# Layer 1's edge stage: float32 one-hots for the expansion of the destinations' scores, and constant products on TensorE

## The chip, the cores and the metric

One core of one Trainium2 chip runs the whole kernel. The metric is the device time of one execution in microseconds; the time of before is the median of three executions. A measurement of this kernel tells a difference from none at about 0.2%.

## What is computed

The kernel is two layers of a graph network over 6250 nodes and 106250 edges, each layer with experts behind it. The change lies in the graph attention of the second layer (layer 1, eight heads, 32 channels each):

```python
alpha = a_src[src] + a_dst[dst] + a_edge
alpha = leaky_relu(alpha, 0.2)
m = segment_max(alpha, dst)
ea = exp(alpha - m[dst])
den = segment_sum(ea, dst)
msg = xp[src] * (ea / den[dst])
out = segment_sum(msg, dst)
```

The edges are sorted by destination. `a_dst[dst]` is what the change computes in another way.

## The kernel before

The stages of the kernel run one after the other. `stage_l1_edges` (line 2312) takes the edges in 58 rounds of 16 steps (`R`) of 128 edges. Every engine runs its own program over the rounds, in the order in which it is written out by hand, and they meet only at semaphores.

- **GpSimd (POOL)**, line 2471: one indirect DMA per step gathers the rows of the 128 sources (256 values with a one for each head, 264 in all, and 8 scores) into `got`, a ring of three rounds. Before each fourth gather it waits until the sums of the same steps three rounds earlier are done (`summed`), which frees their part of the ring.
- **ScalarE (ACT)** makes one-hot matrices: `hot_t` (lines 2495 and 2499, four pieces of 128x512 a round, bfloat16) has the destination node on the partitions, `hot` (lines 2487 and 2482, float32) the edge.
- **TensorE (PE)** does four kinds of products. `expand` (line 2710) gives every edge its destination's score: `hot_t` times `parts`, 16 a round, in four pieces. `parts` are the scores `to_dst` split into three bfloat16 numbers (`split_in_three`, once at the start), so each product has 24 columns. `sums` (line 2721) adds the weighted rows by destination, 16 a round in four pieces, float32, 264 columns. `hop` 0 to 3 (lines 2729, 2732, 2735, 2740 and 2742) are the small products and transposes on the path of the segment maximum.
- **VectorE (DVE)**: `score` (lines 2576 to 2585) adds the three scores of a round: `base`, the sum over the three parts (`from_dst`, line 2579), the addition (line 2582), the leaky ReLU (line 2585, `one`). `spans`, `chains` and `differences` compute the maxima; `weigh` (line 2628) multiplies the gathered rows of four steps by their weights; `add` (line 2636) takes the sums from PSUM.

The rounds are interleaved on TensorE: in its round p stand the hops of round p, the sums of round p-1 and the expansion for round p+1:

```python
hop_of(0)
sums_of(0)
expand_of(0)
hop_of(1)
sums_of(1)
expand_of(1)
hop_of(2)
sums_of(2)
expand_of(2)
expand_of(3)
sums_of(3)
hop_of(3)
```

Hop 0 waits for `one`, hop 1 for `ends` (the end of `spans`), hop 2 for `c_top` (in `chains`), hop 3 for VectorE and for the exponentials of ScalarE; it gives the weights for which the next round's first `weigh` waits. `sums_of(b)` waits for `weigh(b)`. Layer 0 has an edge stage of the same build (`stage_l0_edges`, line 1188; gathers in line 1372) with the same 928 gathers; the change leaves it alone.

Of the kernel before, what the change touches and what calls it, by code (L numbers as in the profile page):

```python
# [19 lines left out]
BF16 = mybir.dt.bfloat16  # L20
I32 = mybir.dt.int32
ALU = mybir.AluOpType
# [1891 lines left out]
def split_in_three(dve, link, whole, parts):  # L1914

    for k in range(2):
        link.done(dve.tensor_copy(parts[k], whole))
        link.done(dve.tensor_tensor(whole, whole, parts[k], ALU.subtract))
    return dve.tensor_copy(parts[2], whole)
# [392 lines left out]
def stage_l1_edges(nc, T, K, acc):  # L2312
# [10 lines left out]
    with ExitStack() as ctx:  # L2323
# [9 lines left out]
        parts = s.sb("parts", [P, NT, 3, H], BF16)  # L2333
        apart = s.sb("apart", [P, 3, R, P], BF16)
        hot = s.sb("hot", [P, 3, U, P])
        hot_t = s.sb("hot_t", [P, B4, U * P], BF16)
# [12 lines left out]
        from_dst = s.sb("from_dst", [P, R, H])  # L2349
# [21 lines left out]
        pa = s.ps("pa", [P, SUMS, 512])  # L2371
        p_one, p_chain, p_tops = px[:, 0:P], px[0:H, P:P + 2 * R], px[:, 2 * P:2 * P + 2 * R]
# [4 lines left out]
        parts_ready = s.sem("parts_ready")  # L2377
# [172 lines left out]
        def _(dve):  # L2550
            link = Tally(dve, s.sem("dve"))
            link.done(dve.memset(links[:, :, :], -BIG))
# [6 lines left out]
            link.done(split_in_three(dve, link, to_dst[:, :, :], [parts[:, :, k, :] for k in range(3)]))  # L2559
            dve.sem_inc(parts_ready, 1)  # L2560
# [10 lines left out]
            def score(p, k, turn, pair):  # L2571
                dve.wait_ge(got_in[k], 16 * R * (turn + 1))
                if isinstance(p, int) and p == 0:
                    dve.wait_ge(edge_in, 16)
                for n in range(RS):
                    ins = dve.tensor_tensor(base[:, 2 * n:2 * n + 2, :], got[:, k, 2 * n:2 * n + 2, WV:ROW],
                                            edge[:, bass.ds(pair[n] * 2, 2), :], ALU.add)
                dve.wait_ge(expanded, B4 * (p + 1))
                dve.tensor_reduce(from_dst[:, :, :], pd[:, 0:R * 3 * H].rearrange("p (r k h) -> p r h k", k=3, h=H), AX, ALU.add
                                  ).then_inc(dst_taken, 1)  # L2580
                dve.wait_ge(dst_taken, p + 1)
                dve.tensor_tensor(base[:, :, :], base[:, :, :], from_dst[:, :, :], ALU.add).then_inc(based, 1)
                dve.wait_ge(based, p + 1)
                flat = base[:, :, :].rearrange("p r h -> p (r h)")
                dve.scalar_tensor_tensor(one[:, :], flat, 0.2, flat, ALU.mult, ALU.max).then_inc(one_ready, 1)
# [115 lines left out]
        def _(pe):  # L2701
            pe.wait_ge(parts_ready, 1)

            def expand(p, b, tile):
                pe.wait_ge(hot_t_ready, p * B4 + b + 1)
                if b == 0 and not (isinstance(p, int) and p == 0):
                    pe.wait_ge(dst_taken, p)
                for u in range(U):
                    r = b * U + u
                    mm = pe.matmul(pd[:, r * 3 * H:(r + 1) * 3 * H], hot_t[:, b, u * P:(u + 1) * P],  # L2710
                                   parts[:, bass.ds(tile[r // 2], 1), :, :].rearrange("p a k h -> p (a k h)"), start=True, stop=True)
                mm.then_inc(expanded, 1)
# [31 lines left out]
            def round_(p, k, ahead, now_, behind):  # L2744
# [14 lines left out]

                hop_of(0)  # L2760
                sums_of(0)
                expand_of(0)
                hop_of(1)
                sums_of(1)
                expand_of(1)
                hop_of(2)
                sums_of(2)
                expand_of(2)
                expand_of(3)
                sums_of(3)  # L2770
                hop_of(3)
# [1110 lines left out]
```

## Time and profile before

| | |
|---|---|
| median of three executions | 7020.55 us (7016.5 to 7024.07) |
| the profiled execution: its time, its span | 7091.8 us, 7089.9 us |
| TensorE clock granted, mean over the span | 0.798 |
| first and last gather of layer 1's edge stage | 4483.7 us, 5879.6 us |
| first and last leaky ReLU of its rounds (L2585) | 4522.8 us, 5892.9 us |
| last sum taken from PSUM (L2636) | 5918.1 us |

The profiled execution is 71 us (1.0%) above the median of the executions that were only timed. Times in rows are microseconds from the start of the span unless marked ns. A row of a timeline begins with start and duration; at its end stands in brackets how long the engine sat idle before it and what released it. A product of float32 operands leaves two records on PE and two weight loads on PEld, one of bfloat16 leaves one of each. The granted clock is 1.0 at 2.4 GHz and 0.5 at 1.2 GHz.

### The profile page before, as it was taken

Reading aid. Unit: us, or ns where it says so; the run is one execution under the profiler, and the core shown is the slowest. Engines: PE = TensorE matmul, PEld = TensorE weight load, DVE = VectorE, ACT = ScalarE, POOL = GpSimd, SP = SyncE. Lnnn points to the kernel's source line nnn. Section 1 sums busy time; section 2 is a strip of 40 time slices with the busy share of each in tenths; the row PEclk is TensorE's granted clock in tenths of the full one; section 3 lists DMA queues with packets and bytes.
Section 4 is the critical chain, followed back from the end, with each engine's and each line's share of the span. In section 5 each row is a group of like instructions: output and inputs, shape, how many; then the busy total and the mean of one; then the engine's idle time right before and its main releaser. Section 6 shows DMA issues by size and latency. Waiting matters only on the chain. (4 is left out here: it accounts for less than half of the span.)

```text
span 7089.9 us, 85593 instructions
## 1 busy us (share of the span) xinstructions
PE 4861.7 (69%) x21453; PEld 3465.5 (49%) x21454; DVE 3989.0 (56%) x9527; ACT 2604.5 (37%) x4956; POOL 3069.3 (43%) x3260
## 2 busy tenths in 40 slices
PE   4368375777777787477778734355555556999999
PEld 3246134555565577345555523244444434666565
DVE  4248136999999975411221297466666666445443
ACT  0134003555555532033333331355555552222222
POOL 2641605666666567366666400466666661000000
PEclk6568697999989955588898856677777777999999
DMA  1001147888888776322222215444444442000000
GB/s 50 1 0 30 48 161 232 251 248 246 250 247 251 237 188 148 96 62 62 59 54 64 59 58 181 139 125 126 126 126 126 123 126 79 11 10 10 10 10 11
DMA packets 587384, 787.20 MB, mean 111 GB/s; under 512 B 207700, under 2 KB 427323, under 8 KB 586749
## 3 DMA queue, kind: packets, MB, share of 16 engines
q0 software_dynamic: 159136, 383.90, 20.3%
q1 hardware_dynamic: 290173, 351.82, 15.6%
q10 hardware_dynamic: 137972, 50.36, 3.1%
q8 instruction: 34, 0.56, 0.0%
q14 instruction: 69, 0.57, 0.0%
HBM read 634.22 MB, written 158.32 MB: 112 GB/s over the span
## 5 line engine op out<-in xcount | busy, mean ns | idle before, releaser
L1372 POOL DMA_INDIRECT b_got<-tmp_l_table,b_src x928 | 877.5, 946 | 537.7 <-issue 251.8
L2471 POOL DMA_INDIRECT w_got<-tmp_l_table,w_src x928 | 879.4, 948 | 519.6 <-issue 261.1
L3203 POOL DMA_INDIRECT t_got<-tmp_f_table,t_src x672 | 634.2, 944 | 409.8 <-DVE t_sums L3281 204.8
L2721 PE MATMUL w_pa<-w_got,w_hot 128*128 128x264 f32 x1856 | 654.3, 512 | 206.1 <-DVE w_got L2628 111.0
L1616 PE MATMUL b_pk<-b_keys,b_hot_t 128*128 x1856 | 553.0, 450 | 284.9 <-issue 194.8
L2721 PEld LDWEIGHTS w_pa<-w_got,w_hot 128*128 128x128 f32 x1856 | 444.2, 252 | 325.4 <-issue 228.7
L1616 PEld LDWEIGHTS b_pk<-b_keys,b_hot_t 128*128 128x128 f32 x1856 | 388.4, 220 | 379.7 <-issue 320.1
L3654 DVE SCALAR_TENSOR_TENSOR l_accs<-l_po,l_prob,l_accs 128x256 f32 (+1 forms) x392 | 173.5, 480 | 564.1 <-PE l_po L3763 564.1
L3706 ACT ACTIVATE l_h<-l_ph,l_bn 128x896 f32<-128x896 f32 x224 | 245.0, 1096 | 652.9 <-PE l_ph L3753 652.9
L3325 PE MATMUL t_po<-t_w,t_hid 128*128 128x256 f32 x1568 | 411.2, 412 | 107.0 <-issue 76.4
L1631 PE MATMUL b_pa<-b_got,b_hot 128*128 128x260 f32 x1856 | 476.8, 402 | 7.8 <-DVE b_acc L1543 4.9
L3317 PE MATMUL t_ph<-t_xt,t_w 128*128 128x448 f32 x896 | 395.4, 585 | 72.7 <-issue 60.1
L1631 PEld LDWEIGHTS b_pa<-b_got,b_hot 128*128 128x128 f32 x1856 | 376.5, 205 | 87.4 <-issue 20.0
L3325 PEld LDWEIGHTS t_po<-t_w,t_hid 128*128 128x128 f32 x1568 | 315.4, 206 | 171.9 <-issue 113.8
L3753 PE MATMUL l_ph<-l_xt,l_wm 128*128 128x448 f32 x896 | 360.5, 558 | 29.6 <-ACT l_h L3706 29.2
L3753 PE MATMUL l_ph<-l_h,l_wm 128*128 128x448 f32 x896 | 356.6, 552 | 2.3 <-DVE l_logit L3622 2.3
L3763 PE MATMUL l_po<-l_wm,l_h 128*128 128x256 f32 x1568 | 348.1, 379 | 8.8 <-ACT l_h L3706 8.8
L1385 ACT ACTIVATE b_hot_t<-b_spread,const_minus_col 128x512 f32<-128x512 bf16 x232 | 166.1, 716 | 508.2 <-remote 351.1
L3763 PEld LDWEIGHTS l_po<-l_wm,l_h 128*128 128x128 f32 x1568 | 296.9, 190 | 67.1 <-issue 27.6
L2628 DVE TENSOR_TENSOR w_got<-w_got,w_pwf 128x1056 f32<-128x1056 f32 x232 | 289.8, 1249 | 56.6 <-remote 47.5
L3243 ACT ACTIVATE t_hid<-t_ph,t_b 128x896 f32<-128x896 f32 x112 | 112.1, 1005 | 534.6 <-remote 307.2
L1475 DVE TENSOR_TENSOR b_got<-b_pk,b_got 128x1024 f32<-128x1024 f32 x232 | 282.6, 1218 | 44.2 <-remote 33.1
(577 smaller groups left out, 9915.5 us busy)
## 6 DMA issues: line engine op xcount, KB each, us to landing
tmp_g_acc<-b_acc SPq DMA_DIRECT2D x232, 260.0 KB
b_spread<-tmp_g_rel_rows SPq DMA_DIRECT2D x116, 256.0 KB
w_spread<-tmp_g_rel_rows SPq DMA_DIRECT2D x116, 256.0 KB
e_attr<-in_edge_attr ACTq DMA_DIRECT2D x103, 256.0 KB
tmp_f_experts<-t_y SPq DMA_DIRECT2D x28, 896.0 KB
t_spread<-tmp_f_rel_rows SPq DMA_DIRECT2D x174, 128.0 KB
yl_y<-tmp_f_experts SPq DMA_DIRECT2D x20, 896.0 KB, 11.1
b_got<-tmp_l_table,b_src POOLq DMA_INDIRECT x928
```

The lines of the kernel that those rows point to most:

```text
L1372: pool.indirect_dma_start(out=got[:, m % NB, u, :], out_offset=None, in_=T["l0_table"], in_offset=bass.IndirectOffsetOnAxis(ap=src[:, m * ...
L1475: dve.tensor_tensor(q, pk[:, b % 2, :].rearrange("p (u d) -> p u d", u=U), q, ALU.mult).then_inc(multiplied, 1)
L1616: mm = pe.matmul(pk[:, b % 2, u * D:(u + 1) * D], hot_t[:, (at * B4 + b) % HB, u * P:(u + 1) * P], keys[:, bass.ds(tile[u // 2], 1), :], s ...
L1631: mm = pe.matmul(pa[:, n % 2, 0:WV], hot[:, b, v, :], got[:, k, v, D:ROW], start=(u == 0), stop=(u == 1))
L2471: pool.indirect_dma_start(out=got[:, p % 3, u, :], out_offset=None, in_=T["l1_table"], in_offset=bass.IndirectOffsetOnAxis(ap=src[:, p * R ...
L2628: dve.tensor_tensor(rows, rows, w.unsqueeze(3).broadcast_to((P, U, H, V)), ALU.mult).then_inc(rhs_ready, 1)
L2721: mm = pe.matmul(pa[:, (k * RS + n) % SUMS, 0:WV], hot[:, (k * B4 + b) % 3, u - b * U, :], got[:, k, u, 0:WV], start=(u == 2 * n), stop=(u ...
L3203: pool.indirect_dma_start(out=got[:, g % RING, u, :], out_offset=None, in_=T["f_table"], in_offset=bass.IndirectOffsetOnAxis(ap=src[:, g * ...
L3317: mm = pe.matmul(ph[:, f % 2, half, 0:HALF], w1[:, e, a, f * P:(f + 1) * P], xt[:, a, half * HALF:(half + 1) * HALF], start=(a == 0), stop ...
L3325: mm = pe.matmul(po[:, f % 2, t % 2, :], hid[:, e % 2, a, t * P:(t + 1) * P], w2[:, e, a, :], start=(a == 0), stop=(a == FC - 1))
L3753: mm = pe.matmul(ph[:, f, h, 0:HALF], wm[which][:, e, a, f * P:(f + 1) * P], of[:, a, h * HALF:(h + 1) * HALF], start=(a == 0), stop=(a == 1))
L3763: mm = pe.matmul(slot(t), h2[:, e % 2, f, t * P:(t + 1) * P], wm[2][:, e, f, :], start=(f == 0), stop=(f == 1))
```

## The change

It has two parts.

The expansion works on float32 throughout: `hot_t` is a float32 tile, the products take `to_dst` itself as the moving operand (8 columns instead of 24), and `parts`, its splitting at the start and `from_dst` go. VectorE adds the result from PSUM to `base` in one operation where it had a reduction and an addition; the semaphore `based` is signalled after the first additions instead.

And TensorE gets products of a constant bfloat16 tile of ones (`idle`, 128x128 against 128x512) into a PSUM bank of their own, `p_idle`, which nobody reads. `fill(n)` issues n of them; they wait for nothing and signal nothing. By the calls in `round_` there are 13 of them in a round (2, 2, 1, 2, 1, 2, 2 and 1), in each of TensorE's 60 rounds.

```diff
-        parts = s.sb("parts", [P, NT, 3, H], BF16)
-        hot_t = s.sb("hot_t", [P, B4, U * P], BF16)
+        hot_t = s.sb("hot_t", [P, B4, U * P])
-        from_dst = s.sb("from_dst", [P, R, H])
+        p_idle = s.ps("p_idle", [P, 512])
+        idle = s.sb("idle", [P, 512], BF16)
...
+            dve.memset(idle[:, :], 1.0).then_inc(idle_ready, 1)
-            link.done(split_in_three(dve, link, to_dst[:, :, :], [parts[:, :, k, :] for k in range(3)]))
-            dve.sem_inc(parts_ready, 1)
...
+                ins.then_inc(based, 1)
                 dve.wait_ge(expanded, B4 * (p + 1))
-                dve.tensor_reduce(from_dst[:, :, :], pd[:, 0:R * 3 * H].rearrange("p (r k h) -> p r h k", k=3, h=H), AX, ALU.add
+                dve.wait_ge(based, p + 1)
+                dve.tensor_tensor(base[:, :, :], base[:, :, :], pd[:, 0:R * H].rearrange("p (r h) -> p r h", h=H), ALU.add
                                   ).then_inc(dst_taken, 1)
                 dve.wait_ge(dst_taken, p + 1)
-                dve.tensor_tensor(base[:, :, :], base[:, :, :], from_dst[:, :, :], ALU.add).then_inc(based, 1)
-                dve.wait_ge(based, p + 1)
...
-            pe.wait_ge(parts_ready, 1)
+            pe.wait_ge(idle_ready, 1)
+            pe.wait_ge(loaded, 8 * 16)
+            def fill(n):
+                for _ in range(n):
+                    pe.matmul(p_idle[:, :], idle[:, 0:P], idle[:, :], start=True, stop=True)
...
-                    mm = pe.matmul(pd[:, r * 3 * H:(r + 1) * 3 * H], hot_t[:, b, u * P:(u + 1) * P],
-                                   parts[:, bass.ds(tile[r // 2], 1), :, :].rearrange("p a k h -> p (a k h)"), start=True, stop=True)
+                    mm = pe.matmul(pd[:, r * H:(r + 1) * H], hot_t[:, b, u * P:(u + 1) * P],
+                                   to_dst[:, bass.ds(tile[r // 2], 1), :].rearrange("p a h -> p (a h)"), start=True, stop=True)
...
+                fill(2)
                 hop_of(0)
+                fill(2)
                 sums_of(0)
                 expand_of(0)
+                fill(1)
                 hop_of(1)
+                fill(2)
                 sums_of(1)
                 expand_of(1)
+                fill(1)
                 hop_of(2)
+                fill(2)
                 sums_of(2)
                 expand_of(2)
                 expand_of(3)
+                fill(2)
                 sums_of(3)
+                fill(1)
                 hop_of(3)
```

On TensorE, from the start of round 1 to hop 1, before the change (a row is a line of the kernel, the operation, its tiles and its shape; x4 is four in a row; a product is one row whatever records it leaves; in the compiled order `w_` marks tiles of this stage, and the `ISA` row sets an address):

```order
L2415 TENSOR_LOAD w_i_row
L2729 MATMUL w_px<-const_ident,w_one 128x128
L2721 MATMUL w_pa<-w_got,w_hot 128x264 x4
L2710 ISA
L2710 MATMUL w_pd<-w_parts,w_hot_t 128x24 x2
L2710 ISA
L2710 MATMUL w_pd<-w_parts,w_hot_t 128x24 x2
L2732 MATMUL w_px<-w_ends,w_of_head 8x32
```

And after it:

```order
L2415 TENSOR_LOAD w_i_row
L2707 MATMUL w_p_idle<-w_idle 128x512 x2
L2734 MATMUL w_px<-const_ident,w_one 128x128
L2707 MATMUL w_p_idle<-w_idle 128x512 x2
L2726 MATMUL w_pa<-w_got,w_hot 128x264 x4
L2715 ISA
L2715 MATMUL w_pd<-w_to_dst,w_hot_t 128x8 x2
L2715 ISA
L2715 MATMUL w_pd<-w_to_dst,w_hot_t 128x8 x2
L2707 MATMUL w_p_idle<-w_idle 128x512
L2737 MATMUL w_px<-w_ends,w_of_head 8x32
```

Five products of `w_idle` stand on the way from the load of the tiles' numbers to hop 1, and the four products of the expansion have 8 columns instead of 24.

On TensorE, at the end of the same round, from the last pair of expansion products to hop 3, before:

```order
L2710 ISA
L2710 MATMUL w_pd<-w_parts,w_hot_t 128x24 x2
L2721 MATMUL w_pa<-w_got,w_hot 128x264 x4
L2740 MATMUL w_pwf<-w_fade_mat,w_first_hot 128x8
L2742 MATMUL w_pwf<-const_ident,w_exps 128x128
```

And after it:

```order
L2715 ISA
L2715 MATMUL w_pd<-w_to_dst,w_hot_t 128x8 x2
L2707 MATMUL w_p_idle<-w_idle 128x512 x2
L2726 MATMUL w_pa<-w_got,w_hot 128x264 x4
L2707 MATMUL w_p_idle<-w_idle 128x512
L2745 MATMUL w_pwf<-w_fade_mat,w_first_hot 128x8
L2747 MATMUL w_pwf<-const_ident,w_exps 128x128
```

Between `sums_of(2)` and `hop_of(3)` stand three constant products more, and ahead of them eight expansion products in the new form, of which the last two are shown.

On VectorE, in `score`, from the last addition of `base` to the leaky ReLU and the first `weigh`, before:

```order
L2576 ISA
L2576 TENSOR_TENSOR w_base<-w_got,w_edge 128x16
L2579 TENSOR_REDUCE w_from_dst<-w_pd 128x128
L2582 TENSOR_TENSOR w_base<-w_base,w_from_dst 128x128
L2585 SCALAR_TENSOR_TENSOR w_one<-w_base 128x128
L2628 TENSOR_TENSOR w_got<-w_got,w_pwf 128x4x264
```

And after it:

```order
L2575 ISA
L2575 TENSOR_TENSOR w_base<-w_got,w_edge 128x16
L2580 TENSOR_TENSOR w_base<-w_base,w_pd 128x128
L2584 SCALAR_TENSOR_TENSOR w_one<-w_base 128x128
L2627 TENSOR_TENSOR w_got<-w_got,w_pwf 128x4x264
```

The reduction from PSUM is gone, and the addition that is left reads PSUM itself.

## Rows read from the trace of the kernel before

**Rows 1.** The page: span, busy time by engine, one of its costliest groups.

```profile
span 7089.9 us, 85593 instructions
...
PE 4861.7 (69%) x21453; PEld 3465.5 (49%) x21454; DVE 3989.0 (56%) x9527; ACT 2604.5 (37%) x4956; POOL 3069.3 (43%) x3260
...
L1385 ACT ACTIVATE b_hot_t<-b_spread,const_minus_col 128x512 f32<-128x512 bf16 x232 | 166.1, 716 | 508.2 <-remote 351.1
```

**Rows 2.** Windows in three stages (layer 0 edges, layer 1 edges, last experts).

```profile
core 0: us, PE busy (x) PEld busy (x) DVE busy (x) ACT busy (x) POOL busy (x), PEclk, DMA share, GB/s
1400.00:1600.00 200.00, 150.66 (x602) 115.06 (x600) 183.87 (x334) 109.66 (x250) 125.72 (x133) 0.93 0.82 247
5200.00:5400.00 200.00, 109.61 (x474) 80.23 (x474) 122.56 (x366) 109.58 (x250) 125.44 (x133) 0.74 0.46 126
6000.00:6200.00 200.00, 193.47 (x655) 122.36 (x654) 99.32 (x248) 52.84 (x55) 0.00 (x0) 0.97 0.03 10
```

**Rows 3.** Groups of layer 1's edge stage: busy us, mean ns, idle before.

```profile
L2471 POOL DMA_INDIRECT w_got<-tmp_l_table,w_src x915 | 867.2, 948 | 513.7 <-issue 257.5 <-PE w_pa L2721 129.4 <-remote 126.8
...
L2721 PEld LDWEIGHTS w_pa<-w_got,w_hot 128*128 128x128 f32 x1856 | 444.2, 252 | 325.4 <-issue 228.7 <-DVE w_got L2628 8.6
...
L2499 ACT ACTIVATE w_hot_t<-w_spread,const_ones 128x512 bf16<-128x512 bf16 x232 | 167.4, 722 | 38.2 <-DMA e_attr<-in_edge_attr 8.9 <-issue 8.8 <-ACT w_spread L2495 1.5
...
L2710 PEld LDWEIGHTS w_pd<-w_parts,w_hot_t 128*128 128x128 bf16 x928 | 57.6, 108 | 84.3 <-issue 61.9
...
L2579 DVE TENSOR_REDUCE w_from_dst<-w_pd 128x128 f32<-128x384 f32 x58 | 32.3, 557 | 30.4 <-DMA e_attr<-in_edge_attr 29.4 <-issue 0.9
...
L2740 PE MATMUL w_pwf<-w_fade_mat,w_first_hot 8*128 8x8 f32 x116 | 23.2, 270 | 0.0
...
L2582 DVE TENSOR_TENSOR w_base<-w_base,w_from_dst 128x128 f32<-128x128 f32 x58 | 17.0, 293 | 2.0
...
L2590 DVE TENSOR_TENSOR w_now<-w_px,w_early 128x128 f32<-128x128 f32 x58 | 16.3, 281 | 14.6 <-issue 14.5
...
L1917 DVE CAST w_parts<-w_to_dst 128x392 bf16<-128x392 f32 x2 | 1.1, 560 | 0.2
```

**Rows 4.** Gathers of layer 0: line 1372, and the first after its ring had filled.

```profile
L1372 POOL DMA_INDIRECT b_got<-tmp_l_table,b_src x928: 940/946/1112, 1057.8 to 2469.8; - x186
...
1153.00 0.94 POOL L1372 DMA_INDIRECT b_got<-tmp_l_table,b_src  x1 [35.41 <-PE b_pa L1631]
```

**Rows 5.** Gathers of layer 1: line 2471 as a whole.

```profile
L2471 POOL DMA_INDIRECT w_got<-tmp_l_table,w_src x928: 940/946/1129, 4483.7 to 5879.6; - x186
```

**Rows 6.** GpSimd's timeline in layer 1's stage: each gather after a wait, one without.

```profile
4561.88 0.94 POOL L2471 DMA_INDIRECT w_got<-tmp_l_table,w_src  x1 [18.29 <-PE w_pa L2721]
...
5304.49 0.95 POOL L2471 DMA_INDIRECT w_got<-tmp_l_table,w_src  x1 [2.19 <-PE w_pa L2721]
5305.74 0.94 POOL L2471 DMA_INDIRECT w_got<-tmp_l_table,w_src  x1 [0.30 <-issue]
...
5316.38 0.94 POOL L2471 DMA_INDIRECT w_got<-tmp_l_table,w_src  x1 [2.21 <-remote]
...
5328.24 0.94 POOL L2471 DMA_INDIRECT w_got<-tmp_l_table,w_src  x1 [2.07 <-PE w_pa L2721]
```

**Rows 7.** Timeline of TensorE and VectorE at the end of one round.

```profile
5309.78 0.35 PE L2710 MATMUL w_pd<-w_parts,w_hot_t 128*128 x8
...
5309.99 2.03 PE L2721 MATMUL w_pa<-w_got,w_hot 128*128 128x264 f32 x8
...
5311.86 0.43 DVE L2636 TENSOR_TENSOR l_sums<-l_sums,w_pa 128x264 f32 x1 [0.46 <-PE w_pa L2721]
...
5311.95 0.38 PE L2740 MATMUL w_pwf<-w_fade_mat,w_first_hot 8*128 8x8 f32 x2
...
5316.34 0.43 DVE L2636 TENSOR_TENSOR l_sums<-l_sums,w_pa 128x264 f32 x1 [4.06 <-remote]
```

**Rows 8.** Timeline pieces: hop 3, `weigh`, a piece of `sums` at either clock, hop 2.

```profile
5197.43 0.38 PE L2740 MATMUL w_pwf<-w_fade_mat,w_first_hot 8*128 8x8 f32 x2
...
5197.74 0.33 PE L2742 MATMUL w_pwf<-const_ident,w_exps 128*128 128x128 f32 x1
...
5198.81 1.25 DVE L2628 TENSOR_TENSOR w_got<-w_got,w_pwf 128x1056 f32<-128x1056 f32 x1
...
5200.19 2.04 PE L2721 MATMUL w_pa<-w_got,w_hot 128*128 128x264 f32 x8 [0.92 <-issue]
...
5225.58 3.88 PE L2721 MATMUL w_pa<-w_got,w_hot 128*128 128x264 f32 x8 [0.77 <-issue]
...
5237.00 0.63 PE L2735 MATMUL w_px<-w_c_top,w_to_head 8*128 8x32 f32 x2 [4.87 <-DVE w_c_top L2603]
```

**Rows 9.** Two 512-column bfloat16 products of the sort stage: timeline, then the line.

```profile
227.55 0.60 PE L637 MATMUL s_pq<-s_not_below,s_ident 128*128 128x512 bf16 x2
...
L637 PE MATMUL s_pq<-s_not_below,s_ident x128: 379/390/634, 126.0 to 665.5; 128*128 128x512 bf16 x128
```

More of the change, by code:

```diff
@@ L2371, in stage_l1_edges @@
         pa = s.ps("pa", [P, SUMS, 512])
+        p_idle = s.ps("p_idle", [P, 512])
+        idle = s.sb("idle", [P, 512], BF16)
+        idle_ready = s.sem("idle_ready")
         p_one, p_chain, p_tops = px[:, 0:P], px[0:H, P:P + 2 * R], px[:, 2 * P:2 * P + 2 * R]
@@ L2376, in stage_l1_edges @@
         set_up = s.sem("set_up")
-        parts_ready = s.sem("parts_ready")
         spread_in = [s.sem(f"spread_in{h}") for h in range(2)]
```

## The prediction

> **What bounds the kernel now.** I read the views from the whole to the place. The page has no engine at its limit: TensorE is busy for 69% of the span, VectorE for 56%, GpSimd for 43% [rows 1], so the limit has to be read stage by stage. The windows of three stages show that [rows 2]. In the last experts' stage TensorE is busy for 193.47 of 200 us; the change does not touch it. In the edge stage of layer 1 nobody is near his limit: TensorE 109.61, VectorE 122.56, ScalarE 109.58, GpSimd 125.44 us of 200, at a granted clock of 0.74, so TensorE moves between its two levels.
>
> The reader should then compare the first two windows. In layer 0's edge stage VectorE is busy for 183.87 us and TensorE's clock is at 0.93; in layer 1's they are 122.56 and 0.74. Both have 133 gathers on GpSimd in 200 us. The exact pace says the same. A ring holds 48 gathers, and the first gather that had to wait for it starts at 1153.00 in layer 0 and at 4561.88 in layer 1; the last of the 928 start at 2469.8 and 5879.6 [rows 4, 5, 6]. That is (2469.8 - 1153.00) / 879 = 1.498 us a gather in the one stage and (5879.6 - 4561.88) / 879 = 1.499 us in the other, or 24.0 us a round, although the work behind the gathers differs. Without a wait gathers start 1.25 us apart [rows 6], which would be 20.0 us a round; the rest is waiting for TensorE's sums, (129.4 + 126.8) / 58 = 4.4 us a round [rows 3].
>
> The timelines show what kind of wait this is. GpSimd stops after eight gathers for some 2.1 us and the pieces are 11.89 and 11.86 us long, 1.48 us a gather [rows 6]. At the end of one of them TensorE's last piece of sums ends at 5312.02, the second take of VectorE begins only at 5316.34, after 4.06 us of idling, and GpSimd's gather at 5316.38 [rows 7]. Products that the trace has as finished are thus seen by VectorE and by GpSimd 4.3 us later, both at once, when GpSimd has been standing still. I can't say from the rows what holds the signals back. But it goes on while gathers are being issued, and then neither a faster TensorE nor a faster VectorE shortens it.
>
> **The change part by part.** Durations are from the profiled execution (7091.8 us, 1.0% above the median of 7020.55); differences are small enough to be subtracted from either.
>
> VectorE loses the reduction, 557 ns, and one addition of 293 ns from SBUF becomes one from PSUM, for which the addition of `now` (same shape, from PSUM) has 281 ns [rows 3]. With the 0.03 us between dependent operations that is 0.6 us a round, 58 x 0.6 = 35 us if all of it lay on the path, nothing if gathers set the pace. The splitting at the start, five operations of 0.56 us [rows 3], lies under the first 48 gathers and is put at nothing; without that cover it would be 2.8 us. The semaphore `based` moves, but its wait stands behind `expanded`, when its eight additions are done: nothing.
>
> ScalarE writes `hot_t` in float32. Layer 0 has that operation, 716 ns [rows 1], against 722 ns here [rows 3]: nothing.
>
> TensorE pays. A float32 product leaves two records. The two of line 2740, with 128 weight columns and 8 moving ones, span 0.38 us at a mean length of 270 ns, so records start 0.11 us apart at the upper clock [rows 3, 8]; the pair of line 2735 in a slow stretch spans 0.63 us, so I take 0.22 us at the lower. The 32 records of a round then take 3.5 us, or 7.0. The bounds are zero beyond today's cost and the record of `sums`, 2.04 / 8 = 0.26 us or 3.88 / 8 = 0.49 [rows 8]; the load of the weights, not the 264 columns, is what the expansion shares, so I stay with the near row. Today eight products span 0.35 us [rows 7], 0.7 a round. Net: 2.8 us a round more, 6.3 at the lower clock. The weight load's own row agrees in kind, 108 ns in bfloat16 and 252 ns in float32 [rows 3]. The Trainium skill (TensorE: Matmul & The Clock Gate, Weight-path perf modes) says that full-width weights that are not float32 get a fast load and float32 ones do not: it speaks against this part of the change. By its figure for one load, 128 columns / 1.2 = 107 ns, the 32 would take an estimated 3.4 us a round where the rows give 3.5.
>
> The 13 constant products: two of this shape in the sort stage span 0.60 us where the shortest record is 0.379, so they start 0.22 us apart [rows 9]: 2.9 us a round, 5.7 at the lower clock. Most stand ahead of a product that waits anyway.
>
> TensorE is busy for 109.61 / 200 x 24.0 = 13.2 us of a round [rows 2]. It gets 5.7 us more at the upper clock, and gives some back if the clock rises: a piece of `sums` takes 2.04 us there and 3.88 at the lower [rows 8], four pieces a round. Either way it stays below 24.0 us as long as the clock is mostly up.
>
> Sum for the likeliest case: the pace stays with the gathers. Behind the last gather one reduction is left, 0.6 us. If the waits shrink to those of the even pieces, 1.48 for 1.499 us, 879 x 0.017 = 15 us is the most to win; I take a third of that, 5 us. 7091.8 becomes 7086, and 7020.55 becomes 7015.
>
> **The rivals.** *VectorE's time comes through.* Every hop starts from `one`, so a loop bound by VectorE and TensorE together gives back all 0.6 us: 7020.55 - 35 = 6986. For it speaks that GpSimd waits for sums and not VectorE for gathers; against it the equal pace of two stages with unequal VectorE.
>
> *The clock pays.* If the waits are TensorE's slowness, the constant products raise the clock and the round falls to the gathers' own issue, at most 879 x 0.25 = 220 us: 6801. Against it stands the 0.93 clock of layer 0 with 133 gathers in 200 us, as many as at 0.74 [rows 2]. The Trainium skill (same page, Why this matters for your kernels) asks to keep TensorE busy and free of long gaps: by that rule the time would be lower, and the trace agrees on the clock but not on the pace.
>
> *Slower: the way to hop 3.* Between the third piece of sums and hop 3 stand eight expansion products and now three constant ones. The expansion there grows by 16 x 0.11 - 0.35 = 1.4 us, the constant ones are 0.7: hop 3 comes 2.1 us later, 4.5 at the lower clock. Its transpose ends at 5198.07 and the `weigh` that needs it starts at 5198.81 [rows 8]: 0.74 us are free. Beyond that the next round waits: 1.4 to 3.8 us. It decides in rounds in which no held-back signal hides it; if these are a third, 20 x 1.4 to 3.8 = 28 to 76 us, 7070 in the middle. `weigh` is then late, and behind it in VectorE's queue the takes of the sums, `spans` and `chains`, so both sums and gathers.
>
> **How the numbers follow.** The gathers' pace holds: 0.42. VectorE's time comes through: 0.25. The clock pays: 0.04. Hop 3: 0.29. The forecast is 7015 us. What a measurement of this kernel tells from no change is 0.2%, 14 us; the first case can fall 16 us and so gives a part of its chance, 0.08, to faster. Faster 0.37, same 0.34, slower 0.29. The range goes down past 6986 to 6968, for a VectorE gain together with shorter waits, and up to 7080, where hop 3 delays a third of the rounds by nearly the full amount; below and above it I leave 0.2, most of it to the hop 3 case in more rounds and to the clock.
>
> **What would show it.** In the profile after, the reduction is gone and the addition takes 0.28 to 0.29 us; `hot_t` stays near 720 ns; expansion records start 0.11 to 0.13 us apart at the upper clock; the granted clock of the stage is above 0.85. The judge is the pace: the last gather less the first that waited, over 879. At 1.48 to 1.50 us the first case holds; below 1.46 VectorE or the clock was the limit; above 1.52 TensorE has become it, and the row of the first `weigh` of a round would then idle for line 2747. I am wrong if the held-back signals depend on how busy TensorE is, in either direction.

## The result, and the profile after

The changed kernel takes 7056.62 us (7054.18 to 7061.52, 5 executions), the kernel before 7024.07 us (7016.5 to 7035.96, 5 executions) in the same comparison: ratio 1.0033, 95% interval 1.0022 to 1.0045, slower by 33 us. The profiled execution of after took 7054.26 us. That of before, 7091.8 us, was 68 us above this median, and its untouched stages were longer too, so the two traces are compared by pace and by waits, not by their ends.

The windows of after, for the stretches of [rows 2]:

```profile
1400.00:1600.00 200.00, 151.37 (x602) 114.79 (x601) 184.59 (x341) 109.88 (x253) 127.36 (x135) 0.93 0.83 250
5200.00:5400.00 200.00, 150.87 (x727) 112.74 (x726) 120.27 (x363) 109.92 (x253) 127.38 (x135) 0.85 0.46 127
6000.00:6200.00 200.00, 193.47 (x657) 123.08 (x656) 93.66 (x220) 48.16 (x49) 0.00 (x0) 0.97 0.03 9
```

TensorE is busy for 41 us more of 200 than in [rows 2], and its granted clock is 0.85 for 0.74. GpSimd issues 135 gathers where it issued 133, so the pace has hardly moved. The groups of the stage in after, for [rows 3]:

```profile
L2471 POOL DMA_INDIRECT w_got<-tmp_l_table,w_src x882 | 840.7, 953 | 499.1 <-issue 243.3 <-remote 161.5 <-PE w_pa L2726 94.3
L2627 DVE TENSOR_TENSOR w_got<-w_got,w_pwf 128x1056 f32<-128x1056 f32 x232 | 289.9, 1249 | 27.3 <-remote 16.0 <-PE w_pwf L2747 8.7 <-issue 0.7
L2707 PE MATMUL w_p_idle<-w_idle 128*128 128x512 bf16 x765 | 275.3, 427 | 3.1 <-issue 2.7
L2715 PEld LDWEIGHTS w_pd<-w_to_dst,w_hot_t 128*128 128x128 f32 x1824 | 248.0, 203 | 27.0 <-issue 11.7
L2580 DVE TENSOR_TENSOR w_base<-w_base,w_pd 128x128 f32<-128x128 f32 x58 | 16.7, 288 | 241.3 <-DMA e_attr<-in_edge_attr 239.4 <-PE w_pd L2715 0.5
```

The last row is the one to look at. The addition takes 288 ns as forecast, but VectorE idles 241.3 us in front of it: 42.7 us in the first round (below) and (241.3 - 42.7) / 57 = 3.5 us on average in the others. The reduction that stood there idled for 30.4 us in all [rows 3]. The releaser named is a load that ended long before; what the instruction waits for is `expanded`, the signal of TensorE's expansion. Of the wait ahead of `weigh` only 8.7 us are for hop 3.

In one of the steady rounds it looks like this (the last expansion products, a gather, VectorE's addition, the next gather):

```profile
4556.77 1.85 PE L2715 MATMUL w_pd<-w_to_dst,w_hot_t 128*128 x16
...
4564.27 0.95 POOL L2471 DMA_INDIRECT w_got<-tmp_l_table,w_src  x1 [0.30 <-issue]
...
4567.11 0.29 DVE L2580 TENSOR_TENSOR w_base<-w_base,w_pd 128x128 f32<-128x128 f32 x1 [4.68 <-DMA e_attr<-in_edge_attr]
...
4567.48 1.07 POOL L2471 DMA_INDIRECT w_got<-tmp_l_table,w_src  x1 [2.26 <-remote]
```

The expansion ends at 4558.62 and VectorE goes on 8.5 us later, in the pause in which GpSimd itself waits for sums: 1.9 us after one gather ended and 0.4 us before the next begins. The waits have moved rather than grown: over the stage the takes of the sums idled for 179.7 us before and 114.0 after, the copy of `chain` for 86.8 and 30.5.

The signal is latest at the stage's start. The timelines of after (TensorE's last expansion products and the constant ones behind them, GpSimd, VectorE):

```profile
4468.39 3.42 PE L2715 MATMUL w_pd<-w_to_dst,w_hot_t 128*128 x16
...
4471.66 2.29 PE L2707 MATMUL w_p_idle<-w_idle 128*128 128x512 bf16 x5
...
4500.85 0.95 POOL L2471 DMA_INDIRECT w_got<-tmp_l_table,w_src  x1 [0.30 <-issue]
...
4507.95 0.29 DVE L2580 TENSOR_TENSOR w_base<-w_base,w_pd 128x128 f32<-128x128 f32 x1 [42.69 <-DMA e_attr<-in_edge_attr]
...
4525.86 0.95 POOL L2471 DMA_INDIRECT w_got<-tmp_l_table,w_src  x1 [24.06 <-PE w_pa L2726]
```

The expansion ends at 4471.8. VectorE has done all its other work and goes on only at 4507.95, 36 us later. In between GpSimd issues gathers back to back, until the 48th ends at 4501.80 and the ring is full: the signal is seen six us after GpSimd fell silent. In the kernel before (below, the group of `weigh` in the stage first) the first signal was seen in the midst of the gathers, after 13.1 us of idling:

```profile
L2628 DVE TENSOR_TENSOR w_got<-w_got,w_pwf 128x1056 f32<-128x1056 f32 x226 | 282.3, 1249 | 56.3 <-remote 47.5 <-issue 6.9
...
4521.90 0.56 DVE L2579 TENSOR_REDUCE w_from_dst<-w_pd 128x128 f32<-128x384 f32 x1 [13.14 <-DMA e_attr<-in_edge_attr]
```

So the 49th gather starts 84.0 us after the first (4525.86 - 4441.9) where it was 78.2 (4561.88 - 4483.7, [rows 5, 6]): it comes 5.8 us later.

### The profile page after: what moved, and what is told of

The parts are those of the page before. It is cut to its first block and busy times, and to the rows that moved or that the text cites. A ratio compares the mean times of both kernels' runs of the same rounds, so it can differ in the third digit from the quotient of the medians.

```text
span 7052.4 us, 89005 instructions
## 1 busy us (share of the span) xinstructions
PE 5105.9 (72%) x23161; PEld 3650.8 (52%) x23162; DVE 3959.8 (56%) x9465; ACT 2607.3 (37%) x4956; POOL 3081.5 (44%) x3260
## 5 line engine op out<-in xcount | busy, mean ns | idle before, releaser
L1616 PE MATMUL b_pk<-b_keys,b_hot_t 128*128 x1856 | 511.8, 423 | 280.1 <-issue 209.8
L2726 PE MATMUL w_pa<-w_got,w_hot 128*128 128x264 f32 x1856 | 564.6, 456 | 42.8 <-issue 31.7
L1616 PEld LDWEIGHTS b_pk<-b_keys,b_hot_t 128*128 128x128 f32 x1856 | 359.7, 204 | 359.2 <-issue 309.1
L2726 PEld LDWEIGHTS w_pa<-w_got,w_hot 128*128 128x128 f32 x1856 | 411.2, 227 | 200.6 <-issue 100.0
L1631 PE MATMUL b_pa<-b_got,b_hot 128*128 128x260 f32 x1856 | 497.2, 415 | 5.7 <-DVE b_acc L1543 4.3
L2707 PE MATMUL w_p_idle<-w_idle 128*128 128x512 bf16 x780 | 282.3, 431 | 32.9 <-issue 32.6
```

The source lines that it names most:

```text
L1616: mm = pe.matmul(pk[:, b % 2, u * D:(u + 1) * D], hot_t[:, (at * B4 + b) % HB, u * P:(u + 1) * P], keys[:, bass.ds(tile[u // 2], 1), :], s ...
L1631: mm = pe.matmul(pa[:, n % 2, 0:WV], hot[:, b, v, :], got[:, k, v, D:ROW], start=(u == 0), stop=(u == 1))
L2707: pe.matmul(p_idle[:, :], idle[:, 0:P], idle[:, :], start=True, stop=True)
L2726: mm = pe.matmul(pa[:, (k * RS + n) % SUMS, 0:WV], hot[:, (k * B4 + b) % 3, u - b * U, :], got[:, k, u, 0:WV], start=(u == 2 * n), stop=(u ...
```

## The experiments

Each run is compared with the kernel before on the same chip. They fell on several chips, with two levels: the kernel before takes 7020 to 7083 us, or 6241 to 6244 us. I write **slow chip** and **fast chip** for the two. The names stand for what the kernel before took beside the run and for no lasting property: the chip that bears number 2 in the record was fast for `b0_again` and slow, an hour later, for `s3_fill_signals`. Whether a chip changes its level or the number does not name one chip, the record does not tell. Theory 1: signals of TensorE are held back while gathers are issued, so gathers set the pace and the change moves little. Theory 2: the way to hop 3 is longer. Theory 3: VectorE's saving is real and TensorE's added work eats it.

**The kernel before, and its parts, on a fast chip.** `b0_again` is the kernel before unchanged.

> The kernel before, unchanged, profiled once more. All theories expect a ratio within 0.2% of 1. What it is for: the profiled execution of before was 7091.8 us against a median of 7024, that of after 7054.3 against 7057, so the two traces can't be subtracted. In the trace of before the edge stage of layer 1 lasted 1439 us (first row 4479.8, last 5919.1) and the rest of the kernel 5651; in the trace of after 1442 and 5610. If the stage itself is what the change made slower by 33 us, this profile has the stage at about 1409 us. If the stage lasts about 1439 here too, the slowdown is not in it.

6245.9 us against 6244.32, ratio 1.0001 (0.9992 to 1.001). The surprise is the 6244 itself, 11% under the 7024 of the first comparison. What the run was for, whether the stage alone had become longer, it can't answer at this level. Its gathers and one window of its stage:

```profile
L2471 POOL DMA_INDIRECT w_got<-tmp_l_table,w_src x928 | 882.8, 951 | 284.6 <-issue 280.3 <-DMA w_src<-tmp_g_src_t 2.2 <-PE w_pa L2721 2.1
...
4600.00:4800.00 200.00, 120.06 (x560) 89.26 (x560) 147.03 (x440) 130.57 (x300) 151.56 (x160) 0.79 0.56 150
```

A gather takes the same 0.95 us, but GpSimd no longer waits for sums: 2.1 us in the whole stage, where it waited 129.4 + 126.8 us in [rows 3]. It issues 160 gathers in 200 us, 1.25 us apart, where a slow chip issues 133. And the first signal is prompt. At the same place as above:

```profile
3906.24 0.35 PE L2710 MATMUL w_pd<-w_parts,w_hot_t 128*128 x4 [2.18 <-ACT w_hot_t L2499]
...
3906.63 0.56 DVE L2579 TENSOR_REDUCE w_from_dst<-w_pd 128x128 f32<-128x384 f32 x1 [1.17 <-PE w_pd L2710]
```

The expansion ends at 3906.59 and VectorE begins at 3906.63, with gathers being issued all the while. Three variants on the same chip (the edits are shortened; `e3` also makes the splitting one copy and moves `based` as in the change):

```diff
 e1_f32_alone (from the changed kernel):
-                for _ in range(n):
-                    pe.matmul(p_idle[:, :], idle[:, 0:P], idle[:, :], start=True, stop=True)
+                pass
 e2_fill_alone: the kernel before, with fill(n) and its calls as in the change
 e3_one_part (from the kernel before; the scores lose their lower digits):
-        parts = s.sb("parts", [P, NT, 3, H], BF16)
+        parts = s.sb("parts", [P, NT, 1, H], BF16)
-                dve.tensor_reduce(from_dst[:, :, :], pd[:, 0:R * 3 * H]...
+                dve.tensor_tensor(base[:, :, :], base[:, :, :], pd[:, 0:R * H]...
```

> The change without its constant products: fill issues nothing. Theory 1 (the gathers set the pace, TensorE does not matter): within 0.2% of before. Theory 2 (the way from the third piece of sums to hop 3 decides, and the float32 expansion lengthens it by 1.4 us at the upper clock and 3.1 at the lower): slower than before by 20 to 60 us. Theory 3 (VectorE's 0.6 us a round come through and the constant products alone cost): faster by up to 35 us.

> The kernel before with the 13 constant products of a round and nothing else; the expansion stays in bfloat16 with three parts. Theory 1: within 0.2% of before. Theory 2: the three constant products ahead of hop 3 add 0.7 us at the upper clock, which the free 0.74 us nearly hide, and the clock rises: 0 to +20 us, and less than e1_f32_alone costs. Theory 3: slower by 33 us plus the missing 35 us, so about +60.

> VectorE's saving by itself: only the first of the three bfloat16 parts of the destinations' scores is multiplied (so the scores lose their lower digits), the products have 8 columns in bfloat16, and VectorE adds them from PSUM in one operation as in the change; no constant products. Theory 1: within 0.2%. Theories 2 and 3, by which the loop of VectorE and TensorE sets the round: faster by 0.6 us a round, 20 to 35 us.

Ratios 0.9997 (0.9988 to 1.0006), 1.0007 (0.9998 to 1.0016), 0.9992 (0.9983 to 1.0001). Where the gathers' own issue bounds the stage, neither part of the change moves the median by more than 0.1%. The whole change was not run on a fast chip. The same kernels on other fast chips:

> The kernel before with 13 constant products a round (bfloat16 expansion and VectorE's reduction stay). Where the kernel before takes 7020 to 7064 us: the change is 1.0029 and the change without these products 1.0016, so if the two parts add up this is 1.001 to 1.002; if the constant products cost only beside the float32 expansion, 1.000. Where it takes 6244 us: 1.0007 as it was.

> The kernel before with one bfloat16 part in place of three: VectorE has the changed kernel's short way, TensorE keeps its fast weight loads (the scores lose their lower digits). It takes VectorE's saving apart from TensorE's price. Theory 1, held-back signals decide and VectorE waits for them anyway: 0.999 to 1.000 where the kernel before takes 7020 to 7064 us. Theory 3, the saving of 0.6 us a round comes through also beside the gathers, as it did (22 us) with the gathers left out: 0.996 to 0.997; the float32 product would then cost 30 to 40 us and not 11.

> The kernel before with one bfloat16 part in place of three (the scores lose their lower digits), once more, for a chip on which the kernel before takes 7020 to 7064 us. If VectorE's saving of 0.6 us a round comes through beside the gathers as it did with the gathers left out (22 us): 0.996 to 0.997, and the float32 product itself then costs 30 to 40 us. If VectorE would only wait longer for a late signal: 0.999 to 1.000.

They gave 0.9998 (0.9989 to 1.0007) for the constant products and 0.999 (0.9981 to 0.9999) and 0.9991 (0.9982 to 1.0) for one part. With the 0.9992 above that is three times some 0.1%, 5 us, for VectorE's saving there, at the edge of what can be measured.

**The change again, and with the gathers left out; a slow chip.** The kernel before takes 7063.66 us here. The edit, shortened:

```diff
 n0_before_no_gathers, n1_after_no_gathers:
                     if p >= 3:
                         pool.wait_ge(summed, RS * (p - 3) + 2 * b + 2)
+                        pool.sem_inc(got_in[p % 3], 16 * U)
+                        continue
...
+                if p < 3:
+                    pool.wait_ge(got_dma[p], 16 * R)
+                    pool.sem_inc(got_in[p], 16 * R)
```

The last lines make GpSimd wait, after each of the first three rounds' 16 gathers, until their rows have landed. That pause is in neither real kernel.

> The change itself, against the kernel before on one chip. Theory 1, held-back signals: what the change costs is later signals from TensorE while gathers are issued. Where the kernel before takes some 7020 us (the gathers of layer 1's edge stage 1.50 us apart) it is 30 us slower, ratio 1.004; where the kernel before takes some 6244 us (gathers 1.25 us apart, so GpSimd never waits) it is the same, within 0.2%. Theory 2, the work itself: the added TensorE work delays a round wherever it runs, so 25 to 35 us on either, ratio 1.004 to 1.005, and gathers more than 1.25 us apart on the chip of 6244 us. Theory 3, VectorE's saving of 0.6 us a round shows: 10 to 35 us faster where signals are prompt.

> The change without the constant products (the float32 expansion and VectorE's shorter way stay). Where the kernel before takes 7020 us: if the second weight load and product of each float32 expansion is what delays, all of the 30 us stay, ratio 1.004; if the constant products do it, 1.000 or a little below for VectorE's 0.6 us a round. Where the kernel before takes 6244 us: 0.9997 as it was, by theory 1.

> The kernel before, with the gathers of rounds 3 to 57 of layer 1's edge stage left out: GpSimd waits for the sums as before and then only raises the semaphore, so the rounds work on old rows and the output is not the reference's. It shows what a round takes when no gather is issued. VectorE is busy for 122.56 of 200 us at 24.0 us a round, 14.7 us a round. Theory 1: TensorE's signals are prompt then, and a round falls to 16 to 18 us on any chip: 6590 to 6700 where the kernel before takes 7020, 6040 to 6130 where it takes 6244. Rival: the 24.0 us of a round come from TensorE's and VectorE's own chain, and then the round stays above 22 us where the kernel before takes 7020.

> The changed kernel, with the same gathers left out in the same way (output not the reference's). Beside the same edit of the kernel before it gives the change's own price with nothing hidden by gathers. If the round is VectorE's chain: 0.6 us a round less, 35 us faster than that one. If TensorE's added 5.7 us a round lie on the path (the way to hop 3, 2.1 us a round, or the expansion that the next round's scores wait for): 1 to 3 us a round more, 58 to 170 us slower than that one.

| | median | ratio to before |
|---|---|---|
| `a1_again`, the change | 7084.53 | 1.0029 (1.0019 to 1.0039) |
| `e4_f32_again`, without constant products | 7074.75 | 1.0016 (1.0008 to 1.0025) |
| `n0`, before without gathers | 6676.57 | 0.9451 (0.9438 to 0.9463) |
| `n1`, the change without gathers | 6654.56 | 0.942 (0.9407 to 0.9433) |

The slowdown is there again, and about half of it without the constant products: 11 us of 21, where 1.004 or 1.000 was expected of `e4` and it came out between them. With the gathers of rounds 3 to 57 left out it is gone: the change is 22 us faster. The leaky ReLU, once a round (in the whole stage, then its 50 rounds in the steady part), and a window, first of `n0`, with its first expansion signal:

```profile
L2591 DVE SCALAR_TENSOR_TENSOR w_one<-w_base x58: 291/292/293, 4491.3 to 5471.3; 128x128 f32<-128x128 f32 x58
...
L2591 DVE SCALAR_TENSOR_TENSOR w_one<-w_base x50: 291/292/293, 4609.3 to 5437.6; 128x128 f32<-128x128 f32 x50
...
4600.00:4800.00 200.00, 138.13 (x654) 102.40 (x655) 172.61 (x518) 155.73 (x358) 0.00 (x0) 0.83 0.15 47
...
4490.00 0.36 PE L2716 MATMUL w_pd<-w_parts,w_hot_t 128*128 x4 [2.19 <-ACT w_hot_t L2505]
...
4490.15 0.95 POOL L2474 DMA_INDIRECT w_got<-tmp_l_table,w_src  x1 [0.30 <-issue]
4490.40 0.56 DVE L2585 TENSOR_REDUCE w_from_dst<-w_pd 128x128 f32<-128x384 f32 x1 [1.66 <-issue]
```

and of `n1`, with the wait for the first expansion:

```profile
L2590 DVE SCALAR_TENSOR_TENSOR w_one<-w_base x58: 291/291/293, 4501.3 to 5450.9; 128x128 f32<-128x128 f32 x58
...
L2590 DVE SCALAR_TENSOR_TENSOR w_one<-w_base x50: 291/291/293, 4610.8 to 5418.1; 128x128 f32<-128x128 f32 x50
...
4600.00:4800.00 200.00, 184.20 (x1019) 140.63 (x1034) 171.24 (x526) 158.46 (x364) 0.00 (x0) 1.00 0.15 47
...
4499.85 0.95 POOL L2474 DMA_INDIRECT w_got<-tmp_l_table,w_src  x1 [0.30 <-issue]
...
4500.96 0.29 DVE L2586 TENSOR_TENSOR w_base<-w_base,w_pd 128x128 f32<-128x128 f32 x1 [19.02 <-DMA e_attr<-in_edge_attr]
...
4503.70 0.94 POOL L2474 DMA_INDIRECT w_got<-tmp_l_table,w_src  x1 [2.90 <-issue]
```

A round takes (5471.3 - 4491.3) / 57 = 17.19 us in `n0` and (5450.9 - 4501.3) / 57 = 16.66 us in `n1`. The first rounds spoil that comparison, since the first 48 gathers are still issued in them. In the steady part it is (5437.6 - 4609.3) / 49 = 16.90 and (5418.1 - 4610.8) / 49 = 16.48 us: without gathers VectorE is busy for 86% of the time, and 0.43 of its 0.6 us a round come through, 25 us in 58 rounds. If VectorE's 0.6 us are right, TensorE's added work costs 0.17 us a round here, though it is busy for 184 of 200 us.

The first rounds show two things. In `n0`, on this slow chip, the first signal is seen 0.04 us after the product's end (4490.36, 4490.40) while gathers are issued, so not every signal is late beside them. In `n1` VectorE waits 19 us for it, 11.8 us past the product's end at 4489.14, and goes on 0.16 us after the 32nd gather ended, in the pause that the edit puts there.

**What VectorE's saving is worth beside gathers, and whether the number of signals decides.** Three times the same two kernels:

```diff
 s: the kernel before with the constant products, and
+                    pe.matmul(p_idle[:, :], idle[:, 0:P], idle[:, :], start=True, stop=True).then_inc(filled, 1)
 v (from the kernel before):
-                mm.then_inc(expanded, 1)
+                if b % 2:
+                    mm.then_inc(expanded, 2)
-                    mm.then_inc(summed, 1)
+                    if n % 2:
+                        mm.then_inc(summed, 2)
```

> The 13 constant products again, but each raises a semaphore that nobody waits for, so TensorE sends 30 signals a round instead of 17. If signals are held back one by one while gathers are issued, a round gets longer by some tenths of a us up to 1 us for each of the 13: 3 to 13 us a round, 7240 to 7800 us, where the kernel before takes 7020 to 7064. If what is held back is let go all at once, or if the lateness has to do with TensorE's work and not with its signals, this is the same as the run without signals, within 0.2%. Where the kernel before takes 6244 us: no change, since nothing is held back there.

> The kernel before with 11 of TensorE's signals a round instead of 17: the sums signal once in four products (two tiles at once, so the first take of a pair of tiles starts later), the expansion once in two blocks; no work is left out. If signals are held back one by one: 100 to 300 us faster where the kernel before takes 7020 to 7064 us. If their number does not matter: the same or up to 30 us slower, for the takes that start one tile later. Where the kernel before takes 6244 us: the same, within 0.2%.

> The kernel before with 13 constant products a round, each of which raises a semaphore that nobody waits for: 30 signals of TensorE a round instead of 17, once more, for a chip on which the kernel before takes 7020 to 7064 us. Signals held back one by one: 3 to 13 us a round longer, 7240 to 7800 us. Lateness that has nothing to do with their number: 1.001 to 1.002, as the constant products alone by the difference of the change (1.0029) and the change without them (1.0016).

> The kernel before with 11 of TensorE's signals a round instead of 17 and no work left out, once more, for a chip on which the kernel before takes 7020 to 7064 us. Signals held back one by one: 100 to 300 us faster. If their number does not matter: the same or up to 30 us slower, for the takes that start one tile later.

The first two pairs fell on fast chips: 1.0004 (0.9995 to 1.0013) and 1.0005 (0.9996 to 1.0014) with more signals, 0.9998 (0.9989 to 1.0007) and 1.0 (0.9991 to 1.0009) with fewer. The third pair fell on a slow one, where the kernel before takes 7083.31 us:

> 30 signals of TensorE a round instead of 17, by constant products that each raise a semaphore nobody waits for. On a chip where the kernel before takes 7020 to 7064 us: held back one by one, 3 to 13 us a round longer, 7240 to 7800 us; if their number does not matter, 1.001 to 1.002. On a chip where it takes 6240 us: 1.000, as twice before.

> 11 of TensorE's signals a round instead of 17, no work left out. On a chip where the kernel before takes 7020 to 7064 us: held back one by one, 100 to 300 us faster; if their number does not matter, the same or up to 30 us slower. On a chip where it takes 6240 us: 1.000, as twice before.

> One bfloat16 part in place of three (the scores lose their lower digits): VectorE's saving without the float32 product. On a chip where the kernel before takes 7020 to 7064 us: 0.996 to 0.997 if the saving comes through beside the gathers, 0.999 to 1.000 if VectorE only waits longer for a late signal. On a chip where it takes 6240 us: 0.999, as three times before.

| slow chip | median | ratio to before |
|---|---|---|
| `s3_fill_signals`, 30 signals a round | 7083.08 | 0.9997 (0.9988 to 1.0006) |
| `v3_fewer_signals`, 11 signals a round | 7081.83 | 0.9998 (0.9989 to 1.0007) |
| `e8_one_part`, VectorE's saving alone | 7084.98 | 1.0002 (0.9992 to 1.0012) |

With that the thought that signals are held back one by one has fallen: 11, 17 or 30 a round take the same time. The constant products cost nothing that can be measured when the expansion stays in bfloat16; 1.001 to 1.002 had been expected even if the number of signals did not matter. And VectorE's saving buys nothing beside gathers: by the interval at most 6 us of the 35. The windows show where it went, first of the kernel before, then of `e8`:

```profile
4600.00:5800.00 1200.00, 675.78 (x2800) 492.32 (x2800) 738.57 (x2193) 654.59 (x1499) 757.15 (x800) 0.73 0.46 126
```

```profile
4600.00:5800.00 1200.00, 682.75 (x2799) 497.93 (x2799) 713.69 (x2147) 652.05 (x1489) 756.38 (x798) 0.73 0.47 125
```

VectorE works 24.9 us less in 1200, and GpSimd issues 798 gathers where it issued 800: the whole saving has become idle time.

**The pace, with layer 0 as the yardstick.** (Last gather less the 49th) / 879, in the profiled execution of each on slow chips, and of `b0_again` on a fast one; the differences are of unrounded values. The rows of after and of `a1_again`:

```profile
L1372 POOL DMA_INDIRECT b_got<-tmp_l_table,b_src x928: 943/949/1136, 1041.1 to 2445.6; - x186
...
L2471 POOL DMA_INDIRECT w_got<-tmp_l_table,w_src x928: 942/949/1107, 4441.9 to 5838.2; - x186
```

```profile
L2471 POOL DMA_INDIRECT w_got<-tmp_l_table,w_src x928: 940/947/1090, 4468.7 to 5880.8; - x186
...
4552.67 0.94 POOL L2471 DMA_INDIRECT w_got<-tmp_l_table,w_src  x1 [24.15 <-PE w_pa L2726]
```

| | layer 0 (untouched) | layer 1 | difference |
|---|---|---|---|
| before | 1.498 | 1.499 | +0.001 |
| `v3`, `e8`, `s3` (bfloat16) | 1.500, 1.502, 1.502 | 1.491, 1.500, 1.498 | -0.009, -0.002, -0.004 |
| `e4` (float32) | 1.495 | 1.496 | +0.000 |
| after, `a1` (float32, constant products) | 1.489, 1.495 | 1.493, 1.511 | +0.004, +0.016 |
| `b0_again` (fast chip) | 1.484 | 1.256 | -0.228 |

The four bfloat16 runs have a mean difference of -0.0035, the three float32 ones of +0.007. That is 0.010 us apart, in 879 gathers 9 us, with a scatter as large. Together with the 5.8 us at the start it would be some 15 of the 21 and 33 us that were measured. But `s3` has those 5.8 us too and loses nothing, so this sum is not shown. From the first gather to the last take of the sums the stage lasts 1430 to 1440 us in the four bfloat16 traces and 1436 to 1450 in the three float32 ones, on average 7 us more; where the rest of the slowdown lies the traces do not tell.

## Why the prediction was wrong

**What held.** On a slow chip the pace stayed nearly where it was, 1.49 to 1.51 us. Late signals are real, were read rightly from [rows 7], and occur while gathers are issued. Taking the gathers away brings the round from 24.0 to 17.2 us. Of the 24.0 us the gathers' own issue takes 20.0, so the waits beside them account for 4.0 of these 6.8 us. VectorE's price was right in kind: 0.6 us forecast, 0.43 measured without gathers. So were the durations: addition 288 ns, `hot_t` 722 ns, and eight records of the new expansion in 0.95 us, 0.12 apart, with two constant products in 0.60:

```profile
5268.10 0.95 PE L2715 MATMUL w_pd<-w_to_dst,w_hot_t 128*128 x8
...
5269.37 0.60 PE L2707 MATMUL w_p_idle<-w_idle 128*128 128x512 bf16 x2
```

The clock rose as well, from 0.74 to 0.85 in the window (0.84 over 4600 to 5800, where above 0.85 was forecast). The Trainium skill (TensorE: Matmul & The Clock Gate, Why this matters for your kernels) asks to keep TensorE busy and free of gaps for the sake of its throughput; the trace agrees on the clock, and no time came back by it: `a1_again` is 21 us slower.

The 7056.62 us lie inside the stated range of 6968 to 7080. That is luck: the upper part of the range was there for a delay on the way to hop 3, and the traces show none. One small slip of the sum changes nothing: 1.499 less 1.48 is 0.019 and not 0.017, so 17 us for 15, of which a third is again some 5.

**What failed** is the step of the sum that put the direction down: "the pace stays with the gathers. Behind the last gather one reduction is left, 0.6 us", and shorter waits, for -5 us in all. The change cost +33 and +21 us, and the pace did not fall to 1.48 but was 1.493 and 1.511. The term that was put at nothing is TensorE's added work, 5.7 us a round by the prediction's own price, because TensorE "stays below 24.0 us". Three sub-steps stand behind it.

The start has no term in the sum; only the splitting was looked at, as lying "under the first 48 gathers". They are no cover for a late signal. Either addition by itself carries the first signal to the end of the 48 gathers: VectorE waits 42.7 us for it in after, 42.9 in `e4` and 38.6 in `s3`, and 13.1 in the kernel before, and the 49th gather starts 5.8 us later. That a signal coming a little later misses its last chance before GpSimd is silent is only argued. And `s3` has the same start (its 49th gather 83.8 us after the first) and no measurable loss, so the start alone does not explain the slowdown.

"Neither a faster TensorE nor a faster VectorE shortens it" was taken to hold in the other direction as well. It does for VectorE (`e8`) and for the constant products alone (`s3`). It does not for the float32 expansion: 11 us by `e4`, 21 with the constant products. The wait for `expanded`, 3.5 us a round and new in place, goes with it: 241.3 us in after, 246.0 in `a1_again`, 163.1 in `e4`, 24 to 42 us in `s3`, `v3` and `e8`. That it is the cause is not shown, and this speaks against it: with this wait VectorE does not idle more in all than without it (1200 - 722.36 = 478 us after, 1200 - 713.69 = 486 us in `e8`, in 1200).

The equal pace of the two stages was read as one cause. `b0_again` shows two: on a fast chip layer 0 still takes 1.484 us and layer 1 falls to 1.256. Layer 0's stage has VectorE busy for 92%, layer 1's had room; that VectorE is what bounds layer 0 is a reading of this share and not a test.

**The rivals.** VectorE's time comes through only where no gathers are issued. The clock rose and paid nothing. Hop 3 had the sign right, by luck, and the place wrong: the idle time ahead of `weigh` fell from 56.3 us to 27.3 in the stage, and the wait came at the expansion, a round's beginning instead of its end.

**What stays open.** Why a longer expansion costs 11 us and why the constant products cost 10 more beside it and none alone. The second difference is barely clear of the noise: the intervals, 1.0008 to 1.0025 and 1.0019 to 1.0039, overlap. Whether a signal is late because GpSimd issues or because the gathers' transfers run was not separated either; `n0` takes both away. In the steady round above the transfers end 1.5 us after the gather does (a DMA share of 0.38, then 0.00), and VectorE goes on 0.4 us behind them:

```profile
4503.30:4507.90 4.60, 0.00 (x0) 0.00 (x0) 0.00 (x0) 0.00 (x0) 0.00 (x0) 0.50 0.00 0
4565.20:4566.70 1.50, 0.00 (x0) 0.00 (x0) 0.00 (x0) 1.39 (x5) 0.02 (x1) 0.50 0.38 102
4566.70:4567.10 0.40, 0.00 (x0) 0.00 (x0) 0.00 (x0) 0.40 (x3) 0.00 (x0) 0.50 0.00 0
```

At the stage's start (the first of these rows) 4.6 us without any transfer pass before the signal is seen. The clean test, the last two blocks of the expansion moved ahead of the third piece of sums so that they are signalled first, was not run. Nor was one that keeps the gathers and changes only where GpSimd pauses. And what makes a chip fast or slow is not known from these runs. No version beat the kernel before by more than 0.1%: one part in place of three comes to 0.999 on fast chips and loses digits.

## What to carry to other kernels

When engines idle for a thing that the trace has as finished, ask what the third engine is doing at that moment; here it was GpSimd's gathers, and leaving them out in one run said more than any shift of work between the other two. If a run leaves something out, look whether its edit puts a wait in elsewhere. Work ahead of the first wait of a ring is not hidden merely because the ring is still filling: look at the first rounds apart from the steady ones. And take two stages' equal pace for one cause only after something has moved one of them.

## What the runs showed of the hardware

- On slow chips VectorE can see TensorE's signals late while GpSimd issues gathers back to back. At the stage's start it is 36.1 us after the product's end in after and 38.4 us in `e4`, 6.1 us after GpSimd stopped; in the steady round shown it is 8.5 us, and 1.9 us after the last gather. Not every signal is late: the first of `n0` was seen after 0.04 us on a slow chip. On a fast chip the first of `b0_again` was too, with the same gathers. The number of signals, 11 to 30 a round, makes no difference.
- The same kernel takes 7020 to 7083 us on some chips and 6241 to 6244 on others. The last experts' stage, where GpSimd issues nothing, does not differ: from the last sum taken to the end of the span it is 7089.9 - 5918.1 = 1171.8 us in the trace of before and 6244.0 - 5073.4 = 1170.6 us in that of `b0_again`.
